# Four graph layers on one core: 32 more wait instructions ahead of the loop in VectorE's program

## The chip, the core and the metric

The kernel runs on one core of a Trainium2 chip. A core has five engines, each with a program (instruction stream) of its own, read from memory in order: TensorE (PE in the profile) multiplies matrices, VectorE (DVE), ScalarE (ACT) and GpSimd (POOL) work on tiles, and SyncE (SP) here issues the DMAs. Engines wait for one another through semaphores. The metric is the time of one execution on the device in microseconds; less is better.

## The reference, cut to what matters

`x` holds 128 graphs of 128 nodes with 512 features in f32, and all graphs share one 128 x 128 adjacency `adj`. Four layers follow one another, each `x = layernorm(x + layer(x))`:

```python
x = _layernorm(x + edge(x, adj, adj, b0))             # max over features of relu(A + C - A ...) + bias
x = _layernorm(x + gat(x, W, a, beta, adj))           # masked attention with leaky relu, elu
x = _layernorm(x + (adj @ x) @ weight + bias)         # graph convolution
x = _layernorm(x + mha(x, adj, Wq, bq, Wk, bk, Wv, bv))  # 8 heads of 64, scores masked by adj
```

The large products use f32 values split into a high and a low part, so that each is three TensorE passes.

## The kernel before, in words

Everything but the weights streams through the core graph by graph. The work is a software pipeline: in a *slot*, each engine does one step of every layer, each step for a graph that lies some slots back (`L_EDGE = 0` to `L_OUT = 8`). All five programs are written by the same helper `slots` (L101 to L109). It writes slots 0 to 11 out (a head without a loop), then a hardware loop (`Fori`, L105) whose body holds four slots and which runs 28 turns (slots 12 to 123), and then the last slots written out once more. In each program the loop ends in a compare-and-branch instruction that goes back to the body's first instruction.

VectorE's program stands in the block at L628. Ahead of the first slot it copies the transposed adjacency (L634, L635), waits for the first weight and the attention vector (L638, L639) and computes eight dot products (L645). Then comes `slots(dve, emit)`. In a slot of the loop VectorE first transposes the attention probabilities (L701), then computes the two dot products of the graph attention layer (L688), which TensorE's transpose at L952 waits for. The last instructions of a slot are the variance steps (L664) and the edge bias (L874). L88 and L90 are the lines of the helper that waits for a semaphore; in the loop such a wait needs a register to be computed first.

In the built program before the change, 574 instructions of VectorE stand ahead of the loop's body, the body has 285 (positions 574 to 858, counted from 0), and 511 follow. The other bodies: TensorE 1147 instructions, ScalarE 204 (positions 347 to 550), GpSimd 101, SyncE 111. The first instruction of VectorE's body sets registers (L105), the second does so and waits (L88), the third is the transpose at L701; the last two, 283 and 284, are L105 (count and branch). Counted from the body's first instruction, the row-minimum steps at L672 take positions 123 to 130 and 251 to 258 in its second and fourth slot (the second of their instructions at 125), and the transpose L805 of the fourth slot has position 248.

Of the kernel before, what the change touches and what calls it, by code (L numbers as in the profile page):

```python
# [35 lines left out]
MASKED = -1.0e9 / SCALE  # L36

BLOCK = 32
SCATTER = 16 * (P // BLOCK)
HEAD_ROWS = (slice(0, HEAD), slice(HEAD, P))  # L40

# [70 lines left out]
def graph_layers_kernel(nc, x, adj, l0_b, l1_w, l1_a, l1_beta, l2_w, l2_bias,  # L112
                        wq, bq, wk, bk, wv, bv, out):
    ctx = ExitStack()
    with ctx:
# [6 lines left out]
        def sem(name):  # L122
            return ctx.enter_context(nc.semaphore(name))
# [98 lines left out]
        adj_in, a_in, const_in = sem("adj_in"), sem("a_in"), sem("const_in")  # L222
# [52 lines left out]
        def _(sp):  # L275
# [4 lines left out]
            def scatter(hbm, blocks, landed):  # L280

                for a in range(P // BLOCK):
                    rows = slice(a * BLOCK, (a + 1) * BLOCK)
                    sp.dma_start(hbm.rearrange("n (b r) p -> r (n b) p", r=BLOCK)[:, :, rows],  # L284
                                 blocks[rows, :].rearrange("r (m c) -> r m c", c=BLOCK)).then_inc(landed, 16)

            def gather(tiles, hbm, landed):
                sp.dma_start(tiles, hbm.rearrange("n q p -> q n p")).then_inc(landed, 16)
# [23 lines left out]
            def emit(slot):  # L312
# [17 lines left out]
                if slot.on(L_PV):  # L330

                    slot.wait(sp, pt_scattered, L_PV, each=SCATTER)
                    gather(probs_t[:, :, :, :].rearrange("p c t n -> p (c t) n"), pt_hbm, pt_in)
                if slot.on(L_TR):
# [3 lines left out]

                    slot.wait(sp, xt_scattered, L_TR, each=SCATTER)
                    gather(xt_f[:, :, :], xt_hbm, xt_in)  # L340
# [12 lines left out]
                if slot.on(L_PV):  # L353

                    slot.wait(sp, ot_scattered, L_PV, each=SCATTER)
                    gather(o_norm[:, :, :].rearrange("p g (c e) -> p (g c) e", e=P), ot_hbm, ot_in)
# [272 lines left out]
        def _(dve):  # L629
# [5 lines left out]
            dve.tensor_tensor(adj_t_lo[:, :], att_bank[:, 0:P], adj_t_hi[:, :].bitcast(F32), ALU.subtract)\  # L635
               .then_inc(setup_copied, 1)

            dve.wait_ge(a_in, 16)  # L638
            dve.wait_ge(w_in[0], 16)  # L639
            for k in range(KC):  # L640
# [52 lines left out]
            def emit(slot):  # L693
# [3 lines left out]
                if slot.on(L_PV):  # L697

                    slot.wait(dve, score_exp, L_PV)
                    slot.wait(dve, pt_scattered, L_PV, 1, SCATTER)  # L700
                    dve.transpose(probs_b[:, :], probs[:, 0, :, :, :].rearrange("p c t n -> p (c t n)"))\  # L701
# [62 lines left out]
                if slot.on(L_TR):  # L764

                    slot.wait(dve, x3_done, L_TR)
                    slot.wait(dve, xt_scattered, L_TR, 1, SCATTER)
                    dve.transpose(x3_b[:, :], x3[:, t2, :]).then_inc(x3_b_done, 1)
# [32 lines left out]
                if slot.on(L_PV):  # L801

                    slot.wait(dve, pv_mm, L_PV)
                    slot.wait(dve, ot_scattered, L_PV, 1, SCATTER)
                    dve.transpose(o_t[:, :], rot[3][:, :]).then_inc(o_t_done, 1)  # L805
# [251 lines left out]
```

## Time and profile before

| | us |
|---|---|
| median of 3 runs (lowest to highest) | 2721.7 (2714.52 to 2723.47) |
| the profiled execution, its own time | 2716.73 |
| its span, first to last instruction | 2714.9 |
| outside the span | 1.8 |
| TensorE busy | 2508.3 |
| VectorE busy | 2067.5 |
| mean granted clock of TensorE | 0.963 |

The profiled execution is 5.0 us below the median of the runs and inside their range. The span is what the views divide up. "PEclk" is the granted clock of TensorE as a share of its full 2.4 GHz: 1.0 is 2.4 GHz and 0.5 is 1.2 GHz. "issue" as a releaser means that the engine stood idle and waited for nothing that the profile shows. The queue "q14 instruction" carries instruction fetches, not data.

### The profile page before, as it was taken

The numbers are of one execution on the slowest core, as the hardware profiler recorded it, in microseconds if no ns is written. First come the engines' busy times: TensorE is split into PE (matmuls) and PEld (weight loads), VectorE is DVE, ScalarE is ACT, GpSimd is POOL, SyncE is SP. The second block draws the span as 40 slices with busy tenths as digits, with TensorE's granted clock in tenths as the row PEclk, the third lists the DMA queues.
The fourth block names the chain that finished last, engine by engine and source line by source line (L and its number), as shares of the span: only waits on it lengthen the run. The fifth ranks groups of instructions, "written<-read, shape, count | busy, mean of one in ns | idle before, by whom it ended". The sixth has DMA issues, their size and how long they took to land. (4 is left out here: it accounts for less than half of the span.)

```text
span 2714.9 us, 58787 instructions
## 1 busy us (share of the span) xinstructions
PE 2508.3 (92%) x17545; PEld 2225.8 (82%) x17545; DVE 2067.5 (76%) x6421; ACT 1335.8 (49%) x4104; POOL 1510.6 (56%) x1806
## 2 busy tenths in 40 slices
PE   3799999999999999999999999999999999999994
PEld 2588888888888888888888888888888888888883
DVE  5678777877778877778878778877778777778852
ACT  3355455555455555555545455545545544455532
POOL 4656555555555655555655555655555655556631
PEclk8899999999999999999999999999999999999996
DMA  3166555655555655555555555655555655556554
GB/s 121 39 138 137 123 131 126 135 132 129 126 129 127 135 130 132 124 129 131 130 130 132 124 132 129 138 125 137 118 129 132 133 123 132 123 132 143 122 127 98
DMA packets 1383046, 343.72 MB, mean 127 GB/s; under 512 B 1084880, under 2 KB 1347152, under 8 KB 1382864
## 3 DMA queue, kind: packets, MB, share of 16 engines
q1 hardware_dynamic: 1382864, 342.05, 56.0%
q14 instruction: 160, 1.31, 0.2%
q8 instruction: 22, 0.36, 0.1%
HBM read 174.13 MB, written 167.77 MB: 126 GB/s over the span
## 5 line engine op out<-in xcount | busy, mean ns | idle before, releaser
L383 POOL TENSOR_TENSOR ve<-mv,eps_col 128x1 f32<-128x1 f32 (+1 forms) x448 | 129.6, 289 | 586.1 <-DVE mv L664 586.1
L887 PE MATMUL rot<-w_hi,y_hi 128*128 128x512 f32 x1024 | 418.7, 409 | 6.9 <-DVE y_lo L730 6.0
L889 PE MATMUL rot<-w_hi,y_lo 128*128 128x512 f32 x1024 | 403.8, 394 | 0.0
L888 PE MATMUL rot<-w_lo,y_hi 128*128 128x512 f32 x1024 | 403.5, 394 | 0.0
L508 ACT ACTIVATE probs<-score,sc_nmax 128x128 f32<-128x128 f32 x1024 | 363.2, 383 | 30.3 <-DVE sc_nmax L672 30.2
L413 POOL TENSOR_TENSOR x2b<-x,bias 128x512 f32<-128x512 f32 x128 | 164.7, 1286 | 327.2 <-DVE x L759 327.2
L887 PE MATMUL rot<-xt_hi,wk_hi 128*128 128x256 f32 x1024 | 319.1, 312 | 0.0
L888 PE MATMUL rot<-xt_lo,wk_hi 128*128 128x256 f32 x1024 | 307.6, 300 | 0.0
L889 PE MATMUL rot<-xt_hi,wk_lo 128*128 128x256 f32 x1024 | 307.4, 300 | 0.0
L887 PE MATMUL rot<-xt_hi,wq_hi 128*128 128x256 f32 x1024 | 300.3, 293 | 0.2 <-DVE xt_lo L860 0.2
L408 POOL TENSOR_TENSOR x<-x,o_norm 128x512 f32<-128x512 f32 x128 | 165.7, 1294 | 241.5 <-DVE o_norm L715 241.5
L388 POOL TENSOR_TENSOR rs<-ve,half_neg 128x1 f32<-128x1 f32 (+1 forms) x448 | 297.5, 672 | 0.6
L888 PE MATMUL rot<-xt_lo,wq_hi 128*128 128x256 f32 x1024 | 289.9, 283 | 0.0
L889 PE MATMUL rot<-xt_hi,wq_lo 128*128 128x256 f32 x1024 | 289.3, 282 | 0.0
L672 DVE CUSTOM_DVE_ANT_0 score<-score,mask 128x128 f32<-128x128 f32 x1024 | 262.5, 319 | 0.0
L701 DVE STREAM_TRANSPOSE probs<-probs 128x1024 f32<-128x1024 f32 x128 | 156.1, 1220 | 129.7 <-issue 124.6
L533 ACT ACTIVATE z<-s_bank,s_col 128x128 f32<-128x128 f32 x128 | 47.0, 367 | 411.9 <-PE s_bank L952 411.9
L783 DVE SCALAR_TENSOR_TENSOR r<-rot,x 128x512 f32<-128x512 f32 x128 | 88.7, 693 | 208.3 <-ACT e L569 140.4
L444 POOL TENSOR_SCALAR e<-e 128x512 f32<-128x512 f32 x128 | 245.9, 1921 | 2.5 <-ACT e L569 2.5
L887 PEld LDWEIGHTS rot<-w_hi,y_hi 128*128 128x128 f32 x1024 | 196.3, 192 | 52.5 <-DVE y_lo L730 7.2
L889 PEld LDWEIGHTS rot<-w_hi,y_lo 128*128 128x128 f32 x1024 | 194.4, 190 | 44.7
L508 ACT ACTIVATION_READ_ACCUMULATOR probs<-score,sc_nmax 128x1 f32 x1024 | 229.6, 224 | 0.0
(109 smaller groups left out, 7283.6 us busy)
## 6 DMA issues: line engine op xcount, KB each, us to landing
pt_hbm<-probs SPq DMA_DIRECT2D x512, 128.0 KB, 2.7
probs_t<-pt_hbm SPq DMA_DIRECT2D x128, 512.0 KB, 4.0
x_in<-in_x SPq DMA_DIRECT2D x128, 256.0 KB, 2.8
xt_hbm<-x_b SPq DMA_DIRECT2D x512, 64.0 KB, 1.9
xt_f<-xt_hbm SPq DMA_DIRECT2D x128, 256.0 KB, 2.8
ot_hbm<-o_t SPq DMA_DIRECT2D x512, 64.0 KB, 2.3
o_norm<-ot_hbm SPq DMA_DIRECT2D x128, 256.0 KB, 2.7
out_x<-x SPq DMA_DIRECT2D x128, 256.0 KB, 2.4
```

Source lines behind the costliest of these rows:

```text
L383: pool.tensor_tensor(ve[n][:, :], var, eps_col[:, 0:1].to_broadcast([P, count]), ALU.add)\
L388: pool.tensor_tensor(rs[n][:, slot.buf(lag, 2) if count == 1 else 0, :], ve[n][:, :], half_neg[:, 0:1].to_broadcast([P, count]), ALU.pow)\
L408: pool.tensor_tensor(res, res, o_norm[:, :, :], ALU.add).then_inc(x4_done, 1)
L413: pool.tensor_tensor(x2b[:, :], x2[:, slot.buf(L_GCN, 2), :], bias2[:, :], ALU.add)\
L444: pool.tensor_scalar(e1[:, :], e1[:, :], 1.0, -1.0, ALU.min, ALU.add)\
L508: ins = act.activation(probs[:, 0, c, t, :], score_tile(c, g, h), ACT.Exp, bias=sc_nmax[:, c, t:t + 1], scale=-1.0, accum_out=sc_sum[:, pa ...
L672: ins = dve.tensor_tensor_reduce(out=tile, in0=tile, in1=mask[:, :], scale=-SCALE, scalar=3.0e38, op0=ALU.add, op1=ALU.min, accum_out=sc_n ...
L701: dve.transpose(probs_b[:, :], probs[:, 0, :, :, :].rearrange("p c t n -> p (c t n)"))\
L783: dve.scalar_tensor_tensor(out=r1[:, g2, :], in0=rot[1][:, :], scalar=0.0, in1=x1[:, slot.buf(L_GAT, 4), :], op0=ALU.max, op1=ALU.add)\
L887: pe.matmul(outp, lh, rh, start=first, stop=False)
L888: pe.matmul(outp, lh, rl, start=False, stop=False)
L889: return pe.matmul(outp, ll, rh, start=False, stop=last)
```

## The change

Between the copy of the adjacency (L635) and the waits for the first weight, VectorE's program gets 64 more calls of `wait_ge` on the semaphore of the adjacency's load. That load has landed long before (the transpose that the adjacency copy waits for has read it), so none of them has anything to wait for. The builder puts two calls into one instruction, which gives 32 instructions.

```diff
 BLOCK = 32
+LOOP_SHIFT = 64
 SCATTER = 16 * (P // BLOCK)
...
             dve.tensor_tensor(adj_t_lo[:, :], att_bank[:, 0:P], adj_t_hi[:, :].bitcast(F32), ALU.subtract)\
                .then_inc(setup_copied, 1)
 
+            for _ in range(LOOP_SHIFT):
+
+                dve.wait_ge(adj_in, 16)
             dve.wait_ge(a_in, 16)
             dve.wait_ge(w_in[0], 16)
```

In the built program VectorE's body now has positions 606 to 890 in place of 574 to 858, with the same 285 instructions; the programs of the other four engines are the same. Instructions that only wait have no row of their own in the order below; they show as the names that the next instruction waits for. VectorE, the first instructions of its program, before:

```order
L628 UNCONDITIONAL_BRANCH [waits barrier_Pool_Activation_PE_DVE_SP_release]
L634 COPY adj_t<-att_bank 128x128 [waits adj_hi_done,setup_mm]
L635 TENSOR_TENSOR adj_t_lo<-att_bank,adj_t_hi 128x128
L645 ISA x,wa_col<-probs,x 128x512 [waits w_in0,a_in]
L645 ISA wa_col 128x1
```

The same place after the change, where the lines are four further on:

```order
L629 UNCONDITIONAL_BRANCH [waits barrier_Pool_Activation_PE_DVE_SP_release]
L635 COPY adj_t<-att_bank 128x128 [waits adj_hi_done,setup_mm]
L636 TENSOR_TENSOR adj_t_lo<-att_bank,adj_t_hi 128x128
L649 ISA x,wa_col<-probs,x 128x512 [waits adj_in,a_in,w_in0]
L649 ISA wa_col 128x1
```

Only the name `adj_in` is new, ahead of the first dot product. The end of the loop's body and the first instructions behind it stand as they were; the body's own beginning, VectorE, is this after the change (before it is the same with L105, L88, L701 and L688):

```order
L106 ISA
L89 ISA [waits score_exp]
L705 STREAM_TRANSPOSE probs<-probs 128x1024 [waits pt_scattered]
L89 REGISTER_ALU
L692 ISA dot_tmp,s_col<-x,u 128x512 [waits x1_done]
```

Nothing in the body is moved against its neighbours.

## Rows read from the trace of the kernel before

**Rows 1.** The page's head, engine totals, and the instruction queue (packets, MB, share).
```profile
span 2714.9 us, 58787 instructions
...
PE 2508.3 (92%) x17545; PEld 2225.8 (82%) x17545; DVE 2067.5 (76%) x6421; ACT 1335.8 (49%) x4104; POOL 1510.6 (56%) x1806
...
q14 instruction: 160, 1.31, 0.2%
```

**Rows 2.** TensorE's waits, 286 to 2482 us (waiter <- releaser: total us, times, longest).
```profile
PE s_bank L952 <- DVE s_col L688: 92.3, 27, 3.7
```

**Rows 3.** VectorE's waits over the same stretch: the longest in total.
```profile
DVE probs L701 <- issue: 124.6, 27, 4.9
```

**Rows 4.** Timeline of VectorE (start us, us, instruction [idle before <-releaser]), 1324 to 1371 us.
```profile
1324.15 1.21 DVE L701 STREAM_TRANSPOSE probs<-probs 128x1024 f32<-128x1024 f32 x1
...
1343.15 1.21 DVE L701 STREAM_TRANSPOSE probs<-probs 128x1024 f32<-128x1024 f32 x1
...
1362.05 0.17 DVE L664 BATCH_NORM_AGGREGATE mv<-st 128x2 f32<-128x6 f32 x1
1367.00 1.25 DVE L701 STREAM_TRANSPOSE probs<-probs 128x1024 f32<-128x1024 f32 x1 [4.78 <-issue]
```

**Rows 5.** VectorE's sequencer on L105, 1361 to 1368 us (duration ns, starts).
```profile
L105 DVEq COMPARE_BRANCH  x1: 68/68/68, 1361.5 to 1361.5; - x1
L105 DVEq FUSED_REGOPS  x1: 63/63/63, 1364.6 to 1364.6; - x1
```

**Rows 6.** VectorE's sequencer on L88, 1361 to 1366.9 us, same columns.
```profile
L88 DVEq FUSED_REGOPS  x1: 46/46/46, 1364.7 to 1364.7; - x1
```

**Rows 7.** Instruction packets (packets, MB, share) in one turn, 1361.4 to 1443.7 us.
```profile
q14 instruction: 5, 0.04, 0.2%
```

**Rows 8.** The same in 0.2 us from 1362.6, 1365.2, 1367.6, 1403.2, 1438.3.
```profile
q14 instruction: 1, 0.01, 18.4%
...
q14 instruction: 1, 0.01, 16.0%
...
q14 instruction: 1, 0.01, 15.6%
...
q14 instruction: 1, 0.01, 26.3%
...
q14 instruction: 1, 0.01, 16.7%
```

**Rows 9.** Timeline of VectorE around the last two of those packets.
```profile
1402.05 0.33 DVE L672 CUSTOM_DVE_ANT_0 score<-score,mask 128x128 f32<-128x128 f32 x1
...
1437.03 0.71 DVE L805 STREAM_TRANSPOSE o_t<-rot 128x512 f32<-128x512 f32 x1
1437.82 0.20 DVE L813 RECIPROCAL sc_inv<-sc_sum 128x8 f32<-128x8 f32 x1
```

**Rows 10.** Stretches: us, busy of five engines (instructions), PEclk, DMA share, GB/s.
```profile
1324.20:1343.20 19.00, 19.00 (x139) 16.93 (x138) 15.43 (x50) 9.52 (x32) 11.24 (x13) 1.00 0.62 133
1367.10:1387.30 20.20, 17.80 (x107) 15.70 (x108) 14.80 (x49) 8.10 (x29) 7.74 (x8) 0.83 0.56 117
2481.70:2557.70 76.00, 76.00 (x551) 67.72 (x550) 64.08 (x203) 41.47 (x128) 47.43 (x57) 1.00 0.60 132
2420.00:2620.00 200.00, 194.98 (x1414) 173.95 (x1413) 159.16 (x487) 102.64 (x317) 118.26 (x141) 1.00 0.59 129
```

**Rows 11.** Starts of L701 that bound the loop's stall turns and the turn after.
```profile
286.26 1.21 DVE L701 STREAM_TRANSPOSE probs<-probs 128x1024 f32<-128x1024 f32 x1
...
2481.71 1.21 DVE L701 STREAM_TRANSPOSE probs<-probs 128x1024 f32<-128x1024 f32 x1
...
2557.68 1.21 DVE L701 STREAM_TRANSPOSE probs<-probs 128x1024 f32<-128x1024 f32 x1
```

**Rows 12.** Timeline of VectorE around the place of the new waits, 3 to 10 us.
```profile
3.80 0.28 DVE L635 TENSOR_TENSOR adj_t_lo<-att_bank,adj_t_hi 128x128 fp32r<-128x128 f32 x1
9.77 0.69 DVE L645 CUSTOM_DVE_ANT_0 x<-probs,x 128x512 f32<-128x512 f32 x1 [5.69 <-DMA probs<-in_L_gnn_W]
```

## The prediction, made before the changed kernel ran

> **What bounds the kernel now.** I read the totals first. TensorE is busy 92% of the span and VectorE 76% [rows 1], so the question is where TensorE's other time goes. Its waits in the looped part name one thing: 27 times it waits at L952 for VectorE's dot products (L688), 92.3 us in all, up to 3.7 us each [rows 2]. The loop has 28 turns and so 27 branches back. VectorE's own waits show the cause one step earlier: 27 times, 124.6 us in all, it stands idle ahead of L701 with "issue" as the releaser, so no semaphore holds it [rows 3]. L701 is the first engine instruction of the loop's body. In the timeline VectorE ends a turn at 1362.2 and starts L701 at 1367.00 after 4.78 us idle; inside a turn, L701 starts at 1324.15 and again at 1343.15 with no such gap [rows 4].
>
> The sequencer's lines say what happens in it. The branch executes at 1361.5, the body's first instruction (L105) at 1364.6, 3.1 us later [rows 5]; the second (L88) follows 0.1 us behind [rows 6], and the third (L701) only at 1367.0, another 2.3 us later [rows 4]. So there are two holes: one between the branch and the body's first instruction, one between its second and its third. The instruction queue has five packets in such a turn [rows 7]: three at 1362.6, 1365.2 and 1367.6, the first two of which fall into the two holes, and two more at 1403.2 and 1438.3 [rows 8]. All packets of this queue have 8 KB (1.31 MB over 160, [rows 1]). The last two fall when VectorE executes positions 125 and 248 of the body (L672 of the second slot, L805 of the fourth) [rows 9] and, if a packet follows its request by the 1.1 us between branch and first packet [rows 5, 8] and the sequencer is 5 to 10 instructions ahead of its engine, when the sequencer passes 130 and 258. That is 128 apart, and 128 before 130 is position 2, the place of the second hole.
>
> So I read the stall thus. Instructions come in blocks of 128. The body's first two instructions are the last two of a block A; then come B (positions 2 to 129), C (130 to 257) and D (258 to 284). On entering a block the sequencer asks for the next one, if it isn't there: entering C fetches D, entering D fetches a fifth block E, which the loop never runs. By the branch, A is gone: it is fetched (first hole), after two instructions B is entered and also has to be fetched (second hole), and entering B fetches C. That makes five packets, as counted. The Trainium skill, "Vector Engine (DVE) Microarchitecture Reference", section 1.2, gives an instruction exactly 64 bytes; 8 KB are then 128 of them, so the packets' size agrees with the distance above.
>
> **The change, part by part.** (1) *Where the blocks' edges fall.* The hole lies ahead of position 574 + 2 = 576 of VectorE's program, so edges are at 576, 704, 832 and 960. After the change the body has positions 606 to 890. Its first block is 576 to 703, its second 704 to 831, its third 832 to 959: three blocks instead of four, and with the one fetched ahead four instead of five. (2) *Do four stay?* Five do not, or there would be no packets in every turn. ScalarE's 204 instructions need at least two blocks plus the one ahead, and in a turn there is no packet beyond the five of VectorE [rows 7], so at least three do stay. The trace does not show whether four do. Both bounds, three and four, are open; I take four, since memories are seldom divided by three. Then no block is fetched after the first turn and both holes go.
>
> The Trainium skill bears on this twice. "Advanced Engine Details and Errata", section "ISA Cache", gives 32 KB to an engine and 128 KB to TensorE; four blocks of 8 KB are 32 KB, which speaks for it, though no run here has shown a size. The opposite reading stands under the rivals.
>
> (3) *What the holes cost.* From the start of L701 at 286.26 to that at 2481.71 are 2195.4 us: 108 slots, 27 turns, each with one stall. From 2481.71 to 2557.68, the turn after the last branch with the same work and no stall, are 75.97 us [rows 11]. 27 x 75.97 = 2051.2 us, so the stalls cost 144.2 us, 5.34 a turn. Of it 92.3 us, 3.4 a turn, is TensorE's wait at L952 [rows 2]; VectorE's 4.6 us gap is longer, since TensorE still has 1.2 us of other work. The rest, 51.9 us or 1.9 a turn, follows from the pause: in the slot behind the stall the granted clock is 0.83 of full speed, so 1.2 GHz for part of it, and the slot takes 20.2 us; a slot without a pause ahead takes 19.0 at 1.00, all of it busy on TensorE [rows 10].
>
> (4) *What is late next.* With the gap gone TensorE is the bound with no wait: 76.00 us busy in the 76.00 us of the turn from 2481.7, and clock 1.00 over the 200 us from 2420, of which only the beginning lies in the loop [rows 10]. So 75.97 a turn is the floor of this loop, and there's nothing further to gain from VectorE, busy 64 of 76 us there.
>
> (5) *The 32 waits themselves.* The semaphore has its value, so each costs only its own issue. The nearest rows are the two sequencer instructions 0.1 us apart [rows 5, 6]: 32 x 0.1 = 3.2 us at most, 0 at least. They stand between L635, ended at 4.08, and L645 at 9.77, and VectorE is idle there for 5.69 us until the weight's DMA lands [rows 12]. The DMA hides them. Without that cover they would cost 3.2 us once. Behind them on VectorE stand only the waits for the same DMA and L645. I take 0.
>
> (6) *Code ahead of and behind the loop.* It is also moved by 32 against the edges. A straight piece enters a block whose fetch was asked for 128 instructions earlier: where D is entered (packet at 1438.3), VectorE goes from L805 to L813 with 0.08 us between [rows 8, 9]. I take 0.
>
> The sum against the profiled execution: 2716.7 - 144.2 + 0 = 2572.5 us. The median of the runs is 5.0 us above that execution. Some of that difference must come from the pauses and the clock behind them, which would be gone, so I add 1.5 and predict **2574 us**, 5.4% below the median.
>
> **Rivals.**
> *One hole stays (storage of three blocks).* For: the trace bounds storage from below at three only. Then the body's first block is still missing after the branch, but 98 instructions stand before the next edge, so the second fetch comes in time. The gap shrinks by 2.3 us (L88 to L701) from 4.6 to 2.3, TensorE's wait from 3.4 to 1.1; with the slow clock behind it between 0 and 1.9 us, a turn costs 1.1 to 3.0 over the floor, 27 turns 30 to 81 us, and the time is 2602 to 2653; I would say 2630. It would show as 27 gaps ahead of L701 of about 2.3 us and four packets a turn.
>
> *Nothing moves.* The edges could lie elsewhere in the changed program (if what the loader puts ahead of it changes too), or the unit that is thrown away could be larger than the packet. Then the two holes stay, and the time is that of before, 2717 to 2722. With a unit of 256 instructions the edges are at 576 or 704 and each 256 from there: the body has 285, crosses one or two of them before and after, and a rule that refetches at each crossing need not gain anything. The five separate packets, the last two 35 us apart [rows 8], speak for 128. By the Trainium skill, "Runtime: NRT & Kernel Launch", section "Instruction fetch mechanics", the instruction memory is two lines of 16 KiB, 256 instructions each, refilled in such blocks; by it this rival would be right. The trace's packets of 8 KB disagree, and the measurement goes first.
>
> *Slower.* If a block were kept only until the next is entered and fetching ahead worked only while the stream ran on from a fetch, the body would have a hole at the branch and at each of its two inner edges (positions 98 and 226): three instead of two. One more hole on VectorE is 2.3 to 3.1 us; TensorE's 1.2 us of other work takes part of it, 1.1 to 1.9 is left, 27 times 30 to 51 us, and up to 51 more by the clock: 2747 to 2819, say 2770. It decides as soon as an inner edge costs over 1.2 us. Against it: the inner edge at 258 costs VectorE nothing today [rows 9].
>
> **How the numbers follow.** Both holes go: 0.84. One stays: 0.08. Nothing moves: 0.05. Slower: 0.03. The likeliest has its own spread: 4.5 us each way from the runs of before, up to 3.2 for the waits, and up to 15 if the granted clock of a TensorE that never pauses falls now and then in 2.1 ms. That is 2564 to 2592, which holds 0.96 of its case and so 0.81 in all; the range needs no more. 0.3% is 8 us, about what a measurement of this kernel tells from no change. The first two cases are faster by more than that (0.92), the third is the same (0.05), and the last is slower (0.03).
>
> **What would show it.** Right: no "issue" gap ahead of L701 in the loop, TensorE's wait at L952 gone there, L701 to L701 18.99 us in all slots, granted clock near 1.00 from 286 us on, about 135 packets fewer in the instruction queue less the first turn's own, and no packet in the middle of a turn. Wrong: four or five packets a turn, gaps ahead of L701, a new gap after positions 98 or 226, or the clock at 0.5 in a stretch where TensorE did not wait. If L645 starts later than 9.8, the waits were not hidden.

## The result, and the profile after

The changed kernel takes 2572.34 us (median of 4 runs, 2571.01 to 2572.94) against 2722.59 us for the kernel before (4 runs, 2714.52 to 2725.63): ratio 0.9452, 95% interval 0.9431 to 0.9473. The forecast was 2574 us in 2564 to 2592. The profiled execution took 2572.94 us; before it was 2716.73, so 143.8 us went, where 144.2 were worked out. In the line numbers of the changed kernel L701 is L705, L688 is L692, L952 is L956, L983 is L987 and L105 is L106.

The page's head, the engines' totals and the instruction queue, after:

```profile
span 2571.2 us, 58819 instructions
...
PE 2459.2 (96%) x17545; PEld 2182.4 (85%) x17545; DVE 2078.4 (81%) x6421; ACT 1337.6 (52%) x4104; POOL 1538.6 (60%) x1806
...
q14 instruction: 25, 0.20, 0.0%
```

TensorE is busy 96% instead of 92% and does the same 17,545 products; the instruction queue moved 25 packets instead of 160 [rows 1]. 27 turns of five are 135, which is the whole difference.

TensorE's waits over the same stretch, 286 to 2482 us (waiter <- releaser: total us, times, longest):

```profile
PE rot L987 <- DMA probs_t<-pt_hbm: 2.7, 2, 1.8
PE rot L972 <- ACT k_sb L500: 1.0, 1, 1.0
```

The wait at L956 for VectorE's dot products, 92.3 us before [rows 2], is gone, and nothing has taken its place. In VectorE's list there is no line for L705 any more [rows 3].

The sequencer on L106 at one branch back (duration ns, start), the first engine instruction behind it, and the packets of all queues between 300 and 2350 us:

```profile
L106 DVEq COMPARE_BRANCH  x1: 56/56/56, 1369.3 to 1369.3; - x1
L106 DVEq FUSED_REGOPS  x1: 63/63/63, 1369.6 to 1369.6; - x1
```

```profile
1369.98 1.21 DVE L705 STREAM_TRANSPOSE probs<-probs 128x1024 f32<-128x1024 f32 x1
```

```profile
q1 hardware_dynamic: 1162367, 283.16, 61.6%
```

The body's first instruction follows the branch by 0.3 us instead of 3.1 [rows 5], and L705 0.4 us later. In these 2050 us of loop only the data queue moved anything: not one instruction packet.

Three stretches (us, busy of the five engines, PEclk, DMA share, GB/s): the loop's 27 turns that had a stall, the turn after, and a slot in the middle:

```profile
286.40:2338.60 2052.20, 2051.30 (x14798) 1827.30 (x14797) 1731.13 (x5401) 1117.85 (x3456) 1280.46 (x1512) 1.00 0.62 138
2338.60:2414.60 76.00, 76.00 (x551) 67.71 (x550) 64.06 (x202) 41.52 (x128) 47.47 (x57) 1.00 0.60 132
1324.20:1343.20 19.00, 19.00 (x141) 16.92 (x137) 15.42 (x50) 11.05 (x33) 11.36 (x14) 1.00 0.68 157
```

27 turns take 2052.2 us, where 27 times the stall-free turn of before [rows 11] gave 2051.2. TensorE is busy in 2051.3 of them at a granted clock of 1.00 throughout [rows 10].

The new waits (duration ns, first and last start), and VectorE's timeline around them:

```profile
L641 DVEq EVENT_SEMAPHORE  x31: 21/50/50, 3.7 to 6.6; - x31
```

```profile
3.81 0.28 DVE L636 TENSOR_TENSOR adj_t_lo<-att_bank,adj_t_hi 128x128 fp32r<-128x128 f32 x1
10.00 0.69 DVE L649 CUSTOM_DVE_ANT_0 x<-probs,x 128x512 f32<-128x512 f32 x1 [5.91 <-DMA probs<-in_L_gnn_W]
```

31 of the waits stand on this line and take 3.0 us, from 3.7 to 6.7, 0.1 us each; the next wait instruction (L642) starts at 6.8. L649 starts at 10.00 instead of 9.77 [rows 12], after the same DMA, which ends the idle time as before. That is later than the 9.8 which the prediction had named as the sign of waits that are not hidden, but the sign was too tight: with the waits behind the loop the first dot product (L646 there) starts at 9.79, with one wait instruction ahead at 9.99 and with two at 10.27. So its start does not follow the number of waits, and at the 32 here they are hidden.

### The profile page after: what moved, and what is told of

Read it like the earlier page. It is cut to its first block, busy times and chain, and to the rows that moved or that the text cites. A ratio compares the mean times of both kernels' runs of the same rounds, so it can differ in the third digit from the quotient of the medians.

```text
span 2571.2 us, 58819 instructions
## 1 busy us (share of the span) xinstructions
PE 2459.2 (96%) x17545; PEld 2182.4 (85%) x17545; DVE 2078.4 (81%) x6421; ACT 1337.6 (52%) x4104; POOL 1538.6 (60%) x1806
## 4 chain that ended last, share of the span: by engine, by line
PE 92%; DMA 3%; DVE 2%; ACT 1%; issue 1%; SPq 1%; POOL 0%; ACTq 0%; DVEq 0%; POOLq 0%
PE rot L891 25%; PE rot L892 24%; PE rot L893 24%; PE score L1000 6%; PE rot L987 5%; PE rot L972 4%; PE rot L941 4%; DMA probs_t<-pt_hbm 1%; DMA pt_hbm<-probs 1%; DVE dot_tmp L692 1%; PE s_bank L956 1%; PE att_bank L1022 1%; SPq L285 0%; ACT probs L509 0%; DVE probs L705 0%
## 5 line engine op out<-in xcount | busy, mean ns | idle before, releaser
L384 POOL TENSOR_TENSOR ve<-mv,eps_col 128x1 f32<-128x1 f32 (+1 forms) x448 | 142.6, 318 | 537.6 <-DVE mv L668 537.5
L389 POOL TENSOR_TENSOR rs<-ve,half_neg 128x1 f32<-128x1 f32 (+1 forms) x448 | 311.0, 702 | 0.6
L891 PE MATMUL rot<-xt_hi,wk_hi 128*128 128x256 f32 x1024 | 299.4, 292 | 0.0
L893 PE MATMUL rot<-xt_hi,wk_lo 128*128 128x256 f32 x1024 | 289.1, 282 | 0.0
L892 PE MATMUL rot<-xt_lo,wk_hi 128*128 128x256 f32 x1024 | 289.1, 282 | 0.0
L892 PEld LDWEIGHTS rot<-w_lo,y_hi 128*128 128x128 f32 x1024 | 195.4, 191 | 33.0
```

The source lines that it names most:

```text
L384: pool.tensor_tensor(ve[n][:, :], var, eps_col[:, 0:1].to_broadcast([P, count]), ALU.add)\
L389: pool.tensor_tensor(rs[n][:, slot.buf(lag, 2) if count == 1 else 0, :], ve[n][:, :], half_neg[:, 0:1].to_broadcast([P, count]), ALU.pow)\
L891: pe.matmul(outp, lh, rh, start=first, stop=False)
L892: pe.matmul(outp, lh, rl, start=False, stop=False)
L893: return pe.matmul(outp, ll, rh, start=False, stop=last)
```

## The experiments

Each kernel was timed in 3 rounds beside the kernel before on the same chip, and its ratio is to that. "Ahead" is in number of wait instructions, each made of two calls.

**The waits at another place.** The same calls, behind the loop.

```diff
-            for _ in range(LOOP_SHIFT):
-                dve.wait_ge(adj_in, 16)
...
             slots(dve, emit)
+            for _ in range(LOOP_SHIFT):
+                dve.wait_ge(adj_in, 16)
```

> The same 64 calls of wait_ge stand behind the loop and the last slots, at the end of VectorE's program, so the body keeps positions 574 to 858. If the body's place is what counts: both holes stay, time as before, 2717 to 2725 us, 27 gaps of about 4.6 us ahead of L701, five instruction packets a turn. If the waits themselves help in some way, by being in the program: about 2572 us.

2720.32 us, ratio 1.0004 (0.998 to 1.0028). VectorE's wait ahead of the transpose, here L702:

```profile
DVE probs L702 <- issue: 125.1, 27, 5.0
```

It is the row of before [rows 3] within 0.5 us. Waits that don't move the body do nothing.

**One instruction ahead.**

```diff
-LOOP_SHIFT = 64
+LOOP_SHIFT = 2
```

> One wait instruction ahead of the loop: body at 575 to 859, edges at 576, 704, 832, so four blocks still, the first with one instruction of the body. Block theory: both holes stay (the second now behind the body's first instruction), time 2717 to 2725 us, five packets a turn. A theory in which any shift or any extra wait at the head changes the loop's timing: less than before.

2718.70 us, ratio 1.0004 (0.9986 to 1.0022). The sequencer behind one branch, first on L106 and then on L89:

```profile
L106 DVEq COMPARE_BRANCH  x1: 68/68/68, 1119.8 to 1119.8; - x1
L106 DVEq FUSED_REGOPS  x1: 63/63/63, 1122.6 to 1122.6; - x1
```

```profile
L89 DVEq FUSED_REGOPS  x1: 46/46/46, 1125.0 to 1125.0; - x1
```

Before, the body's first two instructions ran 0.1 us apart and the hole came behind the second [rows 5, 6]. Now the second (L89) is 2.4 us behind the first: the hole has moved by just one instruction of the body. The edge stays at position 576 of the program, and the body slides over it.

**Two instructions ahead.**

```diff
-LOOP_SHIFT = 64
+LOOP_SHIFT = 4
```

> Two wait instructions ahead of the loop: body at 576 to 860, that is from an edge on, three blocks and one fetched ahead. Block theory with room for four: no gap, 2571 to 2574 us, as with 32. If the gain of 32 waits came from something that grows with their number (a later start of VectorE, another phase against the DMAs): near 2710 us.

2572.87 us, ratio 0.9461 (0.9442 to 0.948), with the range 2570.08 to 2574.41. TensorE's first row over 286 to 2482 us:

```profile
PE rot L987 <- DMA probs_t<-pt_hbm: 2.7, 2, 1.9
```

One instruction more than in the last experiment gives the whole gain, the same as 32. So the number of waits and their time are no part of it.

**128 ahead.**

```diff
-LOOP_SHIFT = 64
+LOOP_SHIFT = 256
```

> 128 wait instructions ahead of the loop: body at 702 to 986, one whole block further than before, two instructions ahead of an edge again. Block theory with units of 128: both holes come back, five packets a turn. Each wait was 0.1 us in the changed kernel, so 12.4 us at the head, of which the weight's DMA hides 5.8: some 6.6 us more than before, 2724 to 2732. With units of 256 instructions this place differs from that of before by half a unit, and the time could be 2580.

2726.34 us, ratio 1.0022 (1.0001 to 1.0044), 6.0 us over the kernel before at its side (2720.37); by the interval it is 0.3 to 12 us. VectorE's wait, and its first dot product:

```profile
DVE probs L705 <- issue: 123.0, 27, 4.8
```

```profile
16.81 0.69 DVE L649 CUSTOM_DVE_ANT_0 x<-probs,x 128x512 f32<-128x512 f32 x1 [12.67 <-issue]
```

The stall is back in full, so the pattern repeats after 128 instructions already, and the unit is not 256. At the branch of 1118.9 us the body's second instruction starts at 1121.8 and L705 at 1124.1, so the second hole lies behind the second instruction again, ahead of position 704. The waits now outlast the weight's DMA: the dot product starts 7.0 us later than before, which agrees with the 6.0.

**101 and 102 ahead.** The body of 285 ends as the last instruction of its third block, or as the first of a fourth.

```diff
-LOOP_SHIFT = 64
+LOOP_SHIFT = 202
```

> 101 wait instructions ahead of the loop: body at 675 to 959, its branch is the last instruction of its third block (edges 704, 832, 960). Block theory: three blocks, no gap, two packets less than five and none per turn. The head costs 101 x 0.097 = 9.8 us less the 5.8 hidden, 4 us: 2574 to 2578 us. The rival that three blocks and one ahead is too tight when the branch stands at the very end: stalls as before, about 2725 us.

2575.56 us, ratio 0.9461 (0.9442 to 0.9479). The instruction queue:

```profile
q14 instruction: 25, 0.20, 0.0%
```

```diff
-LOOP_SHIFT = 64
+LOOP_SHIFT = 204
```

> 102 wait instructions: body at 676 to 960, so that its branch alone lies in a fourth block. Block theory: on entering it a fifth block is asked for, the first is thrown out, and the branch has to fetch it again. 28 instructions stand ahead of the next edge, several us of work, so there is one hole and not two: gap ahead of L701 about 2.4 to 3.1 us, TensorE's wait 1.2 to 1.9 us a turn, clock dip up to 1.9 us: 2576 + 32 to 103 = 2608 to 2679 us, say 2640. Rival: the fifth block's fetch has no time to throw out the first, since the branch comes at once: no gap, 2576 us.

2699.01 us, ratio 0.9911 (0.989 to 0.9933). One instruction costs 123.4 us. Three blocks and the one ahead are kept (no gap, 25 packets); four and the one ahead are not (160 packets). So the room is four blocks, which the trace of before had left open between three and four. The time lies over the forecast of 2608 to 2679, so the size was missed. VectorE's wait, TensorE's waits, and the sequencer at one branch:

```profile
DVE probs L705 <- issue: 95.2, 27, 3.9
```

```profile
PE s_bank L956 <- DVE s_col L692: 63.0, 27, 2.7
PE rot L987 <- DMA probs_t<-pt_hbm: 27.9, 32, 1.8
```

```profile
L106 DVEq ALU_OP  x1: 40/40/40, 1113.8 to 1113.8; - x1
L106 DVEq COMPARE_BRANCH  x1: 68/68/68, 1114.2 to 1114.2; - x1
L106 DVEq FUSED_REGOPS  x1: 63/63/63, 1117.8 to 1117.8; - x1
```

The instruction queue in the half microsecond from 1114.9 us of that branch:

```profile
q14 instruction: 2, 0.02, 15.1%
```

**112 ahead.** 18 instructions of the body stand ahead of its first inner edge.

```diff
-LOOP_SHIFT = 64
+LOOP_SHIFT = 224
```

> 112 wait instructions: body at 686 to 970, 18 instructions ahead of the first inner edge, 11 in the fourth block. Block theory: one hole (between branch and first instruction), since the 18 instructions take some 5 us and the next block comes in 2.4: gap ahead of L701 about 2.4 to 3.1 us, five packets a turn, 2577 + 32 to 103 us, say 2640, as with 102. If a second hole opens behind the 18th instruction, TensorE waits twice and the time is near that of before, 2700 to 2725.

2637.79 us, ratio 0.9691 (0.9672 to 0.9709). The same three views:

```profile
DVE probs L705 <- issue: 68.6, 27, 2.8
```

```profile
PE s_bank L956 <- DVE s_col L692: 36.4, 27, 1.6
PE rot L987 <- DMA probs_t<-pt_hbm: 16.7, 28, 1.0
```

```profile
L106 DVEq ALU_OP  x1: 40/40/40, 1092.3 to 1092.3; - x1
L106 DVEq COMPARE_BRANCH  x1: 68/68/68, 1092.4 to 1092.4; - x1
L106 DVEq FUSED_REGOPS  x1: 63/63/63, 1095.3 to 1095.3; - x1
```

This is the case of one hole by itself: 2.9 us from the branch to the first instruction, and none behind it. VectorE's gap is 68.6 / 27 = 2.5 us instead of 4.6. With the branch as the fourth block's only instruction it follows the count (ALU_OP) by 0.4 us instead of 0.1, the hole behind it is 3.6 us and the gap 3.5. That holds at all 27 branches: the hole is 2.9 to 3.4 us with 112 ahead and 3.5 to 4.1 with 102. The row of the queue shows two packets under way in that half microsecond. I read them as the block ahead, asked for on entering the fourth, and the body's first block, which waits behind that useless one; no row names what a packet carries, and no run took the one away alone.

TensorE's waits are 36.4 + 16.7 = 53.1 us with 112 ahead, of the 61 us that the kernel costs over 101 ahead (62.2, less 11 waits of 0.1 us). With 102 they are 63.0 + 27.9 = 90.9 of 123.4. The remainder is 8 us there and 32 here. It stands in TensorE's busy time, over the 27 turns of the kernel with 112 ahead and then of that with 102:

```profile
291.90:2403.80 2111.90, 2058.80 (x14799) 1827.81 (x14798) 1723.01 (x5401) 1116.31 (x3456) 1253.68 (x1512) 1.00 0.60 135
```

```profile
289.20:2463.60 2174.40, 2082.24 (x14798) 1849.78 (x14797) 1722.54 (x5401) 1116.31 (x3456) 1253.40 (x1513) 0.99 0.59 131
```

That is 7.5 and 30.9 us more than the 2051.3 of the changed kernel, for the same products. The clock makes a part of it. In the 20 us behind L705 (L701) the granted clock was 1.00 in all 27 turns with 112 ahead, where TensorE pauses 1.3 us at L956. With 102 and pauses of 2.3 us it was 1.00 in 12 turns and 0.91 in 15. In the kernel before, with 3.4 us, it was 1.00 in 5, 0.91 in 12 and 0.83 in 10, so the slot of [rows 10] is not typical. Even at 1.00 a turn with a stall has some 76.3 us of busy time and not 76.0; no run shows why.

What the slow clock costs is seen by comparing turns, each from one stalled transpose to the next. Two of the kernel before:

```profile
1691.50:1771.50 80.00, 76.25 (x548) 67.70 (x548) 63.85 (x201) 41.35 (x128) 46.42 (x56) 1.00 0.60 132
1284.80:1367.00 82.20, 78.64 (x548) 70.16 (x548) 63.64 (x200) 41.35 (x128) 46.41 (x56) 0.96 0.57 128
```

And two with 102 ahead:

```profile
957.40:1037.90 80.50, 76.38 (x550) 67.69 (x548) 63.83 (x200) 41.35 (x128) 46.45 (x56) 1.00 0.59 131
877.20:957.40 80.20, 77.67 (x549) 69.19 (x548) 63.72 (x200) 41.34 (x128) 46.40 (x56) 0.98 0.59 131
```

Before, the turns last 80.0 to 80.5 us where the clock stays at 1.00, 80.8 to 81.5 at 0.98 and 81.8 to 82.2 at 0.96. With 102 ahead they last 80.1 to 81.4 us at either clock: where it stays at 1.00, TensorE waits 1.5 to 1.8 us at L987, and where it falls, at most 0.4. There the slow clock only fills time in which TensorE would have waited for the probabilities' load.

**One instruction more in the body.** To part the body's end from its start: 101 ahead and one wait inside.

```diff
+                if not isinstance(slot.base, int) and slot.offset == 2:
+                    dve.wait_ge(adj_in, 16)
+                    dve.wait_ge(adj_in, 16)
                 if slot.on(L_PV):
```

> As with 101 waits ahead (body from 675), and one more wait instruction inside the body, ahead of its third slot, so that it has 286 instructions at 675 to 960. The wait has nothing to wait for and costs 0.1 us a turn beside idle time. If the body's end is what counts (its last instruction in a fourth block): as with 102 waits ahead, 2699 us and five packets a turn. If it is the start (675 is a good one, 676 a bad one): 2576 us.

2696.96 us, ratio 0.9905 (0.9869 to 0.9942). VectorE's wait, here L708:

```profile
DVE probs L708 <- issue: 93.0, 27, 3.8
```

A wait instruction that has nothing to wait for, put into the body, costs 121.4 us over 101 ahead, because it pushes the branch over an edge. The start is the good one of 101 ahead, so it is the number of blocks that decides.

**ScalarE moved as well.**

```diff
+            for _ in range(LOOP_SHIFT):
+                act.wait_ge(const_in, 16 * 6)
             act.wait_ge(const_in, 16 * 6)
```

> The changed kernel, and 32 more wait instructions (on a semaphore that has its value) ahead of the loop in ScalarE's program as well: its body of 204 moves from 347 to 379 and, with edges where TensorE's and VectorE's are (64 past a multiple of 128), it spans three blocks (320 to 447, 448 to 575, 576 to 703) instead of two. Block theory, with the same room of four blocks for ScalarE: no packet more in the loop, 2572 to 2576 us (a few us at the head at most). If ScalarE keeps three only: its loop loses its first block too, three or four packets a turn and ACTIVATE late by 2.4 us a turn, 2600 to 2650 us.

2573.02 us, ratio 0.9453 (0.9419 to 0.9487). The page's head and the queue:

```profile
span 2569.4 us, 58851 instructions
...
q14 instruction: 25, 0.20, 0.0%
```

There is no packet more. If ScalarE's edges lie where VectorE's do, its body now spans three blocks instead of two, and it too keeps three and the one ahead. That is not shown: no run gives the place of its edges, and no shift could be made to fail, since 204 instructions can't span four blocks.

## Why the prediction was right

*What bounds the loop.* VectorE's stall held TensorE up, once a turn. Right: both rows are gone, and TensorE has no wait worth naming for 2050 us.

*Blocks of 128 with edges at 576, 704, 832 and 960.* Right, to the instruction: 574 and 575 stall, 576 does not; 675 does not, 676 does; 702 does again.

*Four stay.* This was the step with the weakest support, a preference between two open bounds, so that it came out right was in part luck. The kernels with 101 and 102 ahead settle it. The Trainium skill, "Advanced Engine Details and Errata", section "ISA Cache", has 32 KB for such an engine, which is four blocks of 8 KB; the runs agree with that total. The same section of the Trainium skill, like its "Runtime: NRT & Kernel Launch", section "Instruction fetch mechanics", has the memory in two lines with 256 instructions each, and that they contradict: with edges 256 apart, at 576 and 832 or at 704 and 960, either the step from 575 to 576 or that from 675 to 676 changes how many blocks the body touches, never both, and 128 ahead would not be the same as none.

*What the holes cost.* Right in the sum: 144.2 against 143.8 us, the pause and the slow clock behind it together. It was taken from the turns' lengths and needed no split. The split was off: 51.9 us were put down to the slow clock. Over the 27 turns of the kernel before, TensorE's busy time is 47.5 us above that of the changed kernel, and beside the 92.3 us it waits 4.3 at L983:

```profile
286.30:2481.70 2195.40, 2098.79 (x14798) 1869.39 (x14797) 1720.15 (x5401) 1116.32 (x3456) 1253.00 (x1513) 0.98 0.58 130
```

```profile
PE rot L983 <- DMA probs_t<-pt_hbm: 4.3, 6, 1.3
```

Without a fall of the clock a stalled turn still lasts 80.0 to 80.5 us, some 4.3 over the floor where 3.4 is the wait at L952. By that, 27 turns would cost some 116 us, and the slow clock adds some 28; both are estimates from the turns above. The floor of 75.97 us a turn held.

*The 32 waits.* Right: 0.1 us each and hidden. With 128 of them the excess over the hiding DMA shows: the first dot product starts 7.0 us later, where 6.6 were expected.

*The 1.5 us for the median.* Not needed: the changed kernel's runs lie within 2 us of each other, and its profiled execution is 0.6 us over their median. The spread belonged to the stalls and the clock behind them: the kernels with both holes ran from 2705 to 2739 us, those without any from 2570 to 2578. In the kernel before, the run of 2705.29 us had a mean granted clock of 0.967 and that of 2732.04 us one of 0.949.

*The rival with one hole* was priced at 30 to 81 us. Its mechanism, in the kernel with 112 ahead, costs 61. Two things were missing in the price of one hole, and they are why 102 ahead fell outside its range. A late L705 delays not just the dot products but also the probabilities' way through memory, so TensorE waits a second time at L987 (16.7 and 27.9 us). And the hole is not of one size: 2.9 to 3.4 us with the branch well inside its block and 3.5 to 4.1 with it just behind an edge.

*Open.* In a turn with a stall all five blocks are fetched, though only the first should be missing. Whether a miss drops everything, or the oldest block goes each time so that each next one is missing when its turn comes, gives the same five packets, and no run tells the two apart. Behind a stall the probabilities' load lands 4.7 to 5.4 us after its issue with 102 ahead, and 4.0 to 4.2 with 112. This goes with the longer wait at L987 (1.5 to 1.8 us at clock 1.00, against 0.5 to 0.7), and no run shows what delays the load. What stands in the 64 places ahead of a program, by which the edges lie at 576 and not at 512 or 640, no row shows.

## What to carry to other kernels

Where an engine stands idle with "issue" as the releaser at the first instruction of a loop's body, once a turn, count the body's instructions and the instruction queue's packets a turn: here, packets in the settled loop meant that its code did not stay. VectorE's body stayed when it touched at most three blocks of 128, so its place counted as well as its length: two idle waits ahead of the loop moved it onto an edge and gave 5.4%. After any edit of such a program look again, since here one instruction more ahead of the branch gave 146 us in one place and cost 123 in another.

## What the runs showed of the hardware that was not expected

A single instruction is worth 146 us here (2718.70 against 2572.87), and 123 at the other edge (2575.56 against 2699.01). The hole after a branch was longer when the branch stood right behind an edge: 3.5 to 4.1 us to the first instruction against 2.9 to 3.4. Pauses of TensorE of 1.3 us left its granted clock at 1.00 in all 27 turns, those of 2.3 us in 12 and those of 3.4 us in 5; in the others the mean over the 20 us behind was 0.91 or 0.83. And a slow clock is not always paid for: with 102 ahead the turns with it are as long as those without, since TensorE then waits less at L987.
